# Layer 2's recurrence on one core: one key difference, one reciprocal for both directions, steps one chunk ahead

## The reference, cut to what matters

```python
def wkv_scan(w, u, k, v):          # over time t, per sequence and feature
    def step(carry, inp):
        a, b, p = carry
        kk, vv = inp
        q = jnp.maximum(p, u + kk)
        e1 = jnp.exp(p - q)
        e2 = jnp.exp(u + kk - q)
        out = (e1 * a + e2 * vv) / (e1 * b + e2)
        q2 = jnp.maximum(p + w, kk)
        f1 = jnp.exp(p + w - q2)
        f2 = jnp.exp(kk - q2)
        return ((f1 * a + f2 * vv, f1 * b + f2, q2), out)
...
r = jax.nn.sigmoid(xn @ Wr.T)
k = xn @ Wk.T
v = xn @ Wv.T
w = -jnp.exp(decay)
wkv_f = wkv_scan(w, u, k, v)
wkv_b = jnp.flip(wkv_scan(w, u, jnp.flip(k, axis=1), jnp.flip(v, axis=1)), axis=1)
wkv = 0.5 * (wkv_f + wkv_b)
x = x + r * wkv @ Wo.T
```

## Time and profile before

| | us |
|---|---|
| median of three runs | 5037.24 (5027.98 to 5040.63) |
| the profiled execution | 5034.39 |
| its span | 5032.6 |
| recurrence, from DVE's first scan to its last `add` | 3783.65 to 4048.00, that is 264.35 |
| PE, DVE, ACT, POOL busy over the span | 3888.0, 2945.0, 1981.6, 984.2 |

### The profile page before, as it was taken

How to read it: one execution, slowest core, us unless ns; L and a number is a source line. 1 busy time by engine, 2 the same in 40 slices (tenths; PEclk the granted TensorE clock), 3 DMA queues, 4 the chain that set the end, 5 groups by cost and what they waited for, 6 DMA issues and landing times. The chain is left out here.

```text
span 5032.6 us, 88050 instructions
## 1 busy us (share of the span) xinstructions
PE 3888.0 (77%) x31066; PEld 2904.1 (58%) x31066; DVE 2945.0 (59%) x5425; ACT 1981.6 (39%) x4245; POOL 984.2 (20%) x904
## 2 busy tenths in 40 slices
PE   7999999999995660799973689799972167866576
PEld 5778777777773440666652356566651045644464
DVE  2555555555555665622234766577778937867682
ACT  2333333333333440133333334487773235643322
POOL 0000000000002110300003156555552242201320
PEclk7999999999998885799996889899985588988567
DMA  3111111111110451200011032222210000000000
GB/s 76 43 48 46 51 43 50 43 51 43 51 43 20 99 120 59 102 1 0 0 29 29 19 135 108 69 69 61 70 41 0 0 5 3 0 12 3 5 0 22
DMA packets 186069, 209.79 MB, mean 42 GB/s; under 512 B 18448, under 2 KB 176112, under 8 KB 178416
## 3 DMA queue, kind: packets, MB, share of 16 engines
q1 hardware_dynamic: 185840, 206.85, 14.1%
HBM read 181.59 MB, written 24.95 MB: 41 GB/s over the span
## 5 line engine op out<-in xcount | busy, mean ns | idle before, releaser
L3450 PE MATMUL c_psO<-c_pt,c_vc 128*128 128x512 f32 x1024 | 482.1, 593 | 2.5 <-ACT c_ot L3537 2.5
L3422 PE MATMUL c_psS<-c_kc,c_qt 128*128 128x257 f32 x2048 | 465.9, 380 | 0.9 <-issue 0.9
L3422 PEld LDWEIGHTS c_psS<-c_kc,c_qt 128*128 128x128 f32 x2048 | 381.2, 190 | 66.8 <-issue 17.4
L3529 ACT ACTIVATE c_sc<-c_psS,c_mx 128x257 f32<-128x257 f32 x512 | 214.9, 472 | 486.5 <-DVE c_mx L3587 486.5
L3576 DVE COPY c_qt<-c_psQ 128x512 f32<-128x512 f32 x248 | 170.7, 688 | 399.7 <-PE c_psQ L3407 399.7
L508 PEld LDWEIGHTS f_psY<-f_w_down,f_hT 128*128 128x128 f32 x2560 | 302.9, 192 | 64.7 <-issue 50.8
L551 ACT ACTIVATE f_hT<-f_psH,f_b_up 128x512 f32<-128x512 f32 x320 | 214.9, 687 | 290.2 <-PE f_psH L498 285.5
L498 PE MATMUL f_psH<-f_xs,f_w_up 128*128 128x512 f32 x640 | 311.2, 623 | 18.5 <-ACT f_hT L551 18.5
L3407 PEld LDWEIGHTS c_psQ<-XT,c_m 128*128 128x128 f32 x1984 | 260.1, 191 | 106.2 <-issue 104.4
L2208 POOL TENSOR_TENSOR x_sc<-x_sc,x_rec 128x1156 f32<-128x1156 f32 x128 | 270.5, 2113 | 224.9 <-DVE x_rec L2474 224.9
L508 PE MATMUL f_psY<-f_w_down,f_hT 128*128 128x128 f32 x2560 | 305.7, 276 | 10.3 <-ACT f_hT L551 7.1
(11 more groups left out here) (711 smaller groups left out, 7976.5 us busy)
## 6 DMA issues: line engine op xcount, KB each, us to landing
c_kc<-in_ctxT SPq DMA_DIRECT2D x128, 257.0 KB, 3.2
c_vc<-in_ctx SPq DMA_DIRECT2D x128, 256.0 KB
g_wide<-g_w_dram SPq DMA_DIRECT2D x32, 1024.0 KB, 8.3
x_kc<-in_ctxT SPq DMA_DIRECT2D x32, 512.0 KB, 3.9
x_vc<-in_ctx SPq DMA_DIRECT2D x64, 256.0 KB
l_k_dram<-l_dist SPq DMA_DIRECT2D x32, 256.0 KB, 3.1
l_q_dram<-l_turn SPq DMA_DIRECT2D x8, 1024.0 KB, 3.9
y_pt<-l_q_dram SPq DMA_DIRECT2D x8, 1024.0 KB, 5.0
```

The lines of the kernel that those rows point to most:

```text
L3422: mm = pe.matmul(psS[:, r, 0:KEYS], qt[:, b // BT, half, b % BT, r * G:(r + 1) * G].rearrange("p h i -> p (h i)"), kc[:, b // 2 % 2, b % 2 ...
L3450: mm = pe.matmul(psO[:], vc[:, slot, c % 2, t, half * P:(half + 1) * P], pt[:, c % 2, t], start=(t == 0), stop=(t == 1))
L3529: act.activation(sc[:, b % 2, r, 0:KEYS], psS[:, r, 0:KEYS], ACT.Exp, bias=mx[:, b % 2, r:r + 1]).then_inc(exp_done, 1)
```

## The change

One difference per chunk, `lead` = pk of the token before minus the key, takes the place of the second maximum, of the bonus add and of the four subtractions: each exponent is exp(-relu(±lead + constant)), so ACT first does four Relus of `lead` (with scale ±1 and a per-feature bias) and then four Exps with scale -1. The products with the values move from POOL to DVE, which leaves POOL its residual adds, now one after each chunk's `add`. The two directions are put over a common denominator: instead of a reciprocal of 992 columns there are three products of 512 (`cross`, `ahead`, `back`), a reciprocal of 512, a sum, the gate, and one more product.

The steps are written out in Python, without hardware loops and without a wait behind every instruction; each consumer waits for its own producer. DVE does `peaks` of chunk j+1, `add` of chunk j-2, `sums` of chunk j and `mix` of chunk j-1. Keys, `lead`, the four exponent tiles, `top`, `low`, `mixed` and psO have two buffers, the gate three. The diff, cut to what the text speaks of:

```diff
@@ -1315,32 +1315,37 @@
...
-        kk = sb("r_kk", [P, WAY, S])
...
+        kk = sb("r_kk", [P, 2, WAY, S])
...
+        lead = sb("r_lead", [P, 2, WAY, S])
...
+        past = sb("r_past", [P, WAY, S])
+        top = sb("r_top", [P, 2, WAY, S])
+        low = sb("r_low", [P, 2, WAY, S])
+        cross = sb("r_cross", [P, BC, S])
...
+        psO = ps("r_psO", [P, 2, CHUNK])
...
-                pe.wait_ge(loaded, 64)
...
-
-                    pe.wait_ge(inputs_ready, j * 6)
+                    if j:
+                        pe.wait_ge(gate_ready, j)
+                        pe.wait_ge(keys_ready, j * 2)
+                        pe.wait_ge(values_ready, j * 2)
...
-                def step(j, p, after):
-                    if after is not None:
-                        project(after)
-                    pe.wait_ge(mix_ready, j + 1 + FREE)
-                    pe.wait_ge(h_added, j)
+                def output(j):
+                    pe.wait_ge(mix_ready, j + 1)
+                    if j >= 2:
+                        pe.wait_ge(h_added, j - 1)
                     for t in range(TC):
-                        mm = pe.matmul(psO[:, t * P:(t + 1) * P], mixed[:, t * P:(t + 1) * P], w_out[:],
+                        mm = pe.matmul(psO[:, j % 2, t * P:(t + 1) * P], mixed[:, j % 2, t * P:(t + 1) * P], w_out[:],
                                        start=True, stop=True)
                     mm.then_inc(out_done, 1)
 
+                pe.wait_ge(loaded, 64)
                 project(0)
-                pairs(pe, step)
+                project(1)
+                for j in range(CHUNKS):
+                    if j + 2 < CHUNKS:
+                        project(j + 2)
+                    if j:
+                        output(j - 1)
+                output(CHUNKS - 1)
...
+                def inputs(j):
+
+                    s = j % 2
+                    act.wait_ge(projected, j * 3 + 3)
+                    if j >= 2:
+                        act.wait_ge(lead_ready, j - 1)
+                    seq = psI[:, 1].rearrange("p (b l) -> p b l", l=S)
+                    act.activation(kk[:, s, 0:BC], seq, ACT.Copy).then_inc(keys_ready, 1)
+                    act.activation(kk[:, s, BC:WAY], seq[:, :, ::-1], ACT.Copy).then_inc(keys_ready, 1)
+                    if j >= 2:
+                        act.wait_ge(e2v_done, j - 1)
+                    seq = psI[:, 2].rearrange("p (b l) -> p b l", l=S)
+                    act.activation(vv[:, s, 0:BC], seq, ACT.Copy).then_inc(values_ready, 1)
+                    act.activation(vv[:, s, BC:WAY], seq[:, :, ::-1], ACT.Copy).then_inc(values_ready, 1)
+                    if j >= 3:
+                        act.wait_ge(mix_ready, j - 2)
+                    act.activation(r_sig[:, j % 3], psI[:, 0], ACT.Sigmoid).then_inc(gate_ready, 1)
+
+                def weights(j):
+
+                    s = j % 2
+                    act.wait_ge(lead_ready, j + 1)
+                    if j >= 2:
+                        act.wait_ge(low_ready, j - 1)
+                        act.wait_ge(top_ready, j - 1)
+                    parts = ((f2, 1.0, w_neg), (f1, -1.0, w_pos), (e2, 1.0, u_neg), (e1, -1.0, u_pos))
+                    for to, sign, by in parts:
+                        act.activation(to[:, s, :, NEXT], lead[:, s, :, NEXT], ACT.Relu, scale=sign, bias=by[:])\
+                            .then_inc(clipped, 1)
+                    for n, (to, sign, by) in enumerate(parts):
+                        act.wait_ge(clipped, j * 4 + n + 1)
+                        act.activation(to[:, s, :, NEXT], to[:, s, :, NEXT], ACT.Exp, scale=-1.0).then_inc(exps, 1)
...
+                act.activation(w_pos[:], decay[:], ACT.Exp).then_inc(decay_ready, 1)
+                inputs(0)
+                act.wait_ge(decay_ready, 1)
+                act.wait_ge(signs_ready, 2)
+                act.wait_ge(firsts_set, 4)
+                weights(0)
+                inputs(1)
+                for j in range(1, CHUNKS):
+                    weights(j)
+                    if j + 1 < CHUNKS:
+                        inputs(j + 1)
...
-                def step(j, p, after):
-                    g.wait_ge(exps, j * 4 + 1)
-                    g.tensor_tensor(f2v[:], f2[:], vv[:, p], ALU.mult).then_inc(products, 1)
-                    g.wait_ge(exps, j * 4 + 3)
-                    g.tensor_tensor(e2v[:, :, 1:S], e2[:, :, 1:S], vv[:, p, :, 1:S], ALU.mult).then_inc(products, 1)
-
-                pairs(g, step)
-
-                with g.Fori(0, CHUNKS) as i:
-                    g.wait_ge(h_added, i + 1)
-                    at = k.X[:, ds(i * CHUNK, CHUNK)]
-                    g.tensor_tensor(at, at, k.H[:, ds(i * CHUNK, CHUNK)], ALU.add).then_inc(x_added, 1)
+                def add(j):
+                    g.wait_ge(h_added, j + 1)
+                    at = k.X[:, j * CHUNK:(j + 1) * CHUNK]
+                    g.tensor_tensor(at, at, k.H[:, j * CHUNK:(j + 1) * CHUNK], ALU.add).then_inc(x_added, 1)
+
+                g.memset(f1[:, :, :, 0:1], 0.0).then_inc(firsts_set, 1)
+                g.memset(f2[:, :, :, 0:1], 1.0).then_inc(firsts_set, 1)
+                g.memset(e2[:, :, :, 0:1], 1.0).then_inc(firsts_set, 1)
+                g.memset(past[:, :, 0:1], 0.0).then_inc(firsts_set, 1)
+                g.memset(low[:, :, :, 0:1], 1.0).then_inc(firsts_set, 1)
+                for j in range(CHUNKS):
...
+                def peaks(j):
+
+                    s = j % 2
...
+                    if j:
+                        v.wait_ge(lead_ready, j)
+                    v.tensor_tensor_scan(pk[:].rearrange(flat), w_step[:].rearrange(flat), kk[:, s].rearrange(flat),
+                                         -1e38, ALU.add, ALU.max).then_inc(peak_done, 1)
+                    if j >= 2:
+                        v.wait_ge(exps, (j - 1) * 4)
+                    v.wait_ge(peak_done, j + 1)
+                    v.tensor_tensor(lead[:, s, :, NEXT], pk[:, :, PREV], kk[:, s, :, NEXT], ALU.subtract)\
+                        .then_inc(lead_ready, 1)
+
+                def sums(j):
+
+                    s = j % 2
+                    v.wait_ge(values_ready, j * 2 + 2)
+                    v.wait_ge(exps, j * 4 + 1)
+                    if j:
+                        v.wait_ge(num_done, j)
+                    v.tensor_tensor(f2v[:], f2[:, s], vv[:, s], ALU.mult).then_inc(f2v_done, 1)
+                    v.wait_ge(exps, j * 4 + 2)
+                    if j:
+                        v.wait_ge(past_den, j)
+                    v.tensor_tensor_scan(den[:].rearrange(flat), f1[:, s].rearrange(flat), f2[:, s].rearrange(flat),
+                                         0.0, ALU.mult, ALU.add).then_inc(den_done, 1)
+                    v.wait_ge(f2v_done, j + 1)
+                    if j:
+                        v.wait_ge(past_num, j)
+                    v.tensor_tensor_scan(num[:].rearrange(flat), f1[:, s].rearrange(flat), f2v[:].rearrange(flat),
+                                         0.0, ALU.mult, ALU.add).then_inc(num_done, 1)
+                    v.wait_ge(exps, j * 4 + 4)
+                    if j:
+                        v.wait_ge(top_ready, j)
+                    v.tensor_tensor(e2v[:], e2[:, s], vv[:, s], ALU.mult).then_inc(e2v_done, 1)
+                    v.wait_ge(den_done, j + 1)
+                    if j >= 2:
...
+                    v.tensor_tensor(low[:, s, :, NEXT], e1[:, s, :, NEXT], den[:, :, PREV], ALU.mult)\
+                        .then_inc(past_den, 1)
+                    v.wait_ge(num_done, j + 1)
+                    v.tensor_tensor(past[:, :, NEXT], e1[:, s, :, NEXT], num[:, :, PREV], ALU.mult)\
+                        .then_inc(past_num, 1)
+                    v.wait_ge(past_den, j + 1)
+                    v.tensor_tensor(low[:, s, :, NEXT], low[:, s, :, NEXT], e2[:, s, :, NEXT], ALU.add)\
+                        .then_inc(low_ready, 1)
+                    v.wait_ge(past_num, j + 1)
+                    v.wait_ge(e2v_done, j + 1)
+                    v.tensor_tensor(top[:, s], past[:], e2v[:], ALU.add).then_inc(top_ready, 1)
...
+                def mix(j):
+                    s = j % 2
+                    other = slice(BC, WAY)
+                    v.wait_ge(low_ready, j + 1)
+                    if j:
+                        v.wait_ge(mix_ready, j)
+                    v.tensor_tensor(cross[:], low[:, s, 0:BC], low[:, s, other, ::-1], ALU.mult).then_inc(crossed, 1)
+                    v.wait_ge(top_ready, j + 1)
+                    v.tensor_tensor(ahead[:], top[:, s, 0:BC], low[:, s, other, ::-1], ALU.mult).then_inc(weighted, 1)
+                    v.tensor_tensor(back[:], top[:, s, other, ::-1], low[:, s, 0:BC], ALU.mult).then_inc(weighted, 1)
+                    v.wait_ge(crossed, j + 1)
+                    v.reciprocal(cross[:], cross[:]).then_inc(inverted, 1)
+                    v.wait_ge(weighted, j * 2 + 2)
```

(78 more changed lines are left out.)

86 lines of the change are left out of this document (31 added, 55 removed).

## The result

| | before | changed |
|---|---|---|
| median of four runs, us | 5036.11 | 4971.69 |
| lowest and highest | 5027.98, 5040.63 | 4968.32, 4974.96 |
| span of the profiled execution | 5032.6 | 4973.1 |
| recurrence, first projection to last `add` | 3773.97 to 4048.00: 274.0 | 3781.86 to 3987.09: 205.2 |

The ratio of the times is 0.988, with a 95% interval from 0.9859 to 0.99: faster by 1.2%, 64 us. The forecast of 4962 us was 10 us low, and its range, 4948 to 4992, holds the result. The stage itself lost 68.8 us, where the sum had 72.2.

What follows compares the result with a forecast made beforehand. DVE, busy 181.35 of 193.50 us, was taken as the bound. Steps of 23.2 us against 32.25, with one 10.3 us idle stretch, gave 5034.39 - 72.2 = 4962.2, forecast as 4962 us; range 4948 to 4992.

Steps and rivals of the forecast that it cites:

- The bound and the step: Recurrence stage: DVE is the bound, and a full step falls from 32.25 to 23.2 us.
- the scans: Den and num in `sums`: 2.2 us each from start to start, chosen over 1.24 and 1.85 us more.
- the reciprocal: In `mix`, 512 columns: 6.24 ns per column gives 3.35 us, charged at 3.27 less the overlap.
- the waits that were put at nothing: In `sums`, waits for instructions at least two back charged nothing; ACT's 12.9 us a step also cost nothing.
- The rival of slow scans: Multiply-add scans den and num stay slow, 3.1 us in each of eight steps: 4987 us, chance 0.13.
- rival 2: DVE's hand-overs cost 0.1 us more on some 16 instructions, 1.6 us a step: 4975 us, chance 0.10.
- a granted PE clock of 0.57: Read in this stage as midway between PE's two levels, 1.2 and 2.4 GHz; PE waits there anyway.
- POOL's adds: One per step beside DVE's f2v and den, costing DVE 0.9 us each, between ends of 0 and 1.26.
- The start: Before the second maximum scan DVE idles 10.3 us once, until ACT copies chunk 1's keys.
- Rivals 3 and 4: ACT's wait repeats each step: fully, 5057 us, chance 0.03; or 3 to 8 us, 4985 to 5020, chance 0.05.
- PE's output [...] must be ready for `add` after `peaks`: 2.2 against 3.42: Each step: PE's eight weight passes, 2.07 us, finish while DVE runs `peaks`, 3.42 us.
- 6 `add` beside other work: Stage total: six of DVE's `add` instructions charged 3.7 us together, with no wait for PE.

Runs made afterwards that it cites:

- the part alone in the kernel before: Products f2v and e2v moved from POOL to DVE, nothing else, against the kernel before: 5028.6 us.
- the three repairs: Against the changed kernel: keys copied ahead of the Exps, POOL's adds under the reciprocal, the last step's add behind sums: 4952.38 us.
- the adds late: Against the changed kernel, POOL's add waits for the next chunk's second weighted product, so it starts under the reciprocal: 4952.6 us.

## Why the prediction was right, and where its 10 us went

**The bound and the step held.** DVE spends 23.31 us a step, 23.2 were worked out. Of the terms, the scans (2.2 from start to start), the reciprocal and the products of 992 columns came out to a few hundredths, as did the waits that were put at nothing. In part the agreement of the step is luck: POOL's add cost 0.17 more than its term and `peaks` 0.08 more (3.50 for 3.42), while `mix` took 7.05 in place of 7.17 and `sums`, without POOL's part, 11.09 in place of 11.13. The rival of slow scans (4987) fell in the profile, and the part alone in the kernel before shows the same from the other side. Hand-overs cost nothing where the awaited instruction is two back (992 columns still come 1.10 apart), so rival 2, with 1.6 us a step, fell too; only those to the very next one cost the lost overlap and 0.03 to 0.04 us more, or 0.11 between the maximum scan and `lead` (3838.27 and 2.28, then 3840.66). One reading was off, and nothing hung on it: a granted PE clock of 0.57, that is some 1.4 GHz, lies near the lower of the two levels and not midway.

**POOL's adds** were put at 0.9 us each, and cost 1.07, between that and their length alone.
The rule of the Trainium skill, "SBUF — State Buffer", section "Who interferes with whom", an exclusive lock, gave up to 1.26. The traces agree with it: den paid 1.08, and the variant with the products on POOL 5.3 us for three instructions of 5.9.
The scans came out alike, as the Trainium skill's "DVE: opcode table, instruction layouts, handler registers and perf-mode slots", section 6, would have it: 2.286, 2.28 and 2.261. Beside 1.22 for a product of the same width, that is close to its half throughput.

**The start** was right: 10.3 us of idle time foreseen, 10.44 found, ended by ACT's keys. Rivals 3 and 4, in which such a wait repeats, did not come: after the second scan DVE never waited for ACT.

**What failed, in the stage: 3.4 us.** The step is "PE's output [...] must be ready for `add` after `peaks`: 2.2 against 3.42". The last step has an `add` and no `peaks`; the cover is gone and 2.17 us are in the open. I had written the sum's "6 `add` beside other work" without asking for each of the six what the other work is. All else between the second scan and the end was 0.5 longer, in small differences like those above. Ahead of the second scan, the first projection took 5.1 us in place of 4.6 (0.5), and the scan came 0.25 later than that explains. The 0.5 of the projection is not the change's: the same code took 4.6 to 5.1 us in the profiles of the variants.

**What was not foreseen, outside the stage.** In the two profiled executions the changed kernel's stage began 7.9 us later, and the stages behind it took 1.5 longer: 68.8 - 7.9 - 1.5 is the 59.4 us of the spans. The code ahead is the same. In eleven profiles, of ten kernels, the stage begins anywhere from 3766.2 to 3781.9. The largest part of that scatter is in Layer 0's mixture stage, which from its first instruction to the first of the stage behind it took 495.9 us at the least and 508.5 at the most. Between the two executions, though, it makes 2.3 of the 7.9 us; the rest comes in small parts from several stages. Against the forecast this counts in full: 4962.2, 3.4 of the stage and 9.4 outside are the 4975.0 of that execution, and the median was 3.3 better. Whether a part of it leans to the changed kernel's side stays open: the medians beside it less 68.8 would be 4967.3 and 4962.7, and the two measured, 4971.7 and 4972.9, lie 4 and 10 us above. Single runs of one kernel spread by up to 16 us, but the means of all runs on record, fifteen before and eight changed, differ by 63.7 us with a standard error of about 2.4, and that is 5 less than the stage gave. The kernel with the three repairs, with the same straight-line code, gained 80.7 us in its mean where its stage gave 82.2, which speaks against a price of that code.

**What the parts are worth**, each undone alone: the look-ahead 31 us, the common denominator 17.5, the clips on ACT 14.7, the products on DVE 12.0. This isn't a division of the 69 us. The clips on DVE are a form that neither kernel has. And no run undid what the rows make the largest term: one `lead` in place of the second maximum and four subtractions. From start to start, those five took 5.7 us in the kernel before and `lead` takes 1.1, so an estimate is 4.6 us a step and 37 in eight. Nor was the wait behind every instruction put back alone. Both are argued from the rows and not shown. The products alone, done first, gave 10 us in the kernel before.

## What to carry to other kernels

Where one engine is busy 94% of a stage, price its instructions one by one from start to start, and look for time that others take from it: a second engine that "relieves" it by reading the same memory can cost more than the work it takes over. Put such an engine's work under instructions that don't collide (here the reciprocal, with one input). When a chain is moved one step ahead, go through the first and the last step by hand, since there the cover is missing: 10.4 and 2.2 us here, of which about 6.5 could be had back.

## What the hardware showed that I had not expected

When POOL's and DVE's two-input instructions meet, the one that starts second is lengthened by nearly what the other still has to run, and it need not be the one beside which POOL's was issued: f2v kept its 1.22 us and the den behind it paid, and in the variant with the clips on DVE a POOL add of 1.26 us stood 4.31 us while f2v and den ran untouched, and num paid with 3.29.

The scatter ahead of the stage goes with the granted PE clock. The same 150 us of the mixture stage, first in the changed kernel's profile, then in the one with the adds late, whose stage began 15.7 us earlier:

```profile
2270.00:2420.00 150.00, 144.72 (x812) 104.01 (x811) 32.81 (x110) 58.31 (x84) 1.23 (x2) 0.98 0.00 0
```

```profile
2270.00:2420.00 150.00, 144.72 (x839) 105.76 (x838) 32.44 (x109) 60.67 (x87) 1.23 (x2) 1.00 0.00 0
```

PE is at its upper level, 2.4 GHz, all the time in the second (1.00) and not quite in the first (0.98), and with the same busy time it gets through 839 instead of 812 matmuls. The other nine profiles fit: the two others with 1.00 in this window (a reciprocal for each direction, and the three repairs together) are the two others whose mixture stage was below 500 us, and the rest have 0.98 and 504.5 to 508.5 us. What makes the difference between the executions, no run here shows.
